# Adding the expert rows into the output in memory by accumulating scatters, with a reordered beginning, in a fused attention and mixture-of-experts kernel

## The reference

```python
x = X                                   # (8, 1024, 128), float32
xn = layernorm(x)
# attention part, per batch and head (16 heads of 64):
q, k, v = xn @ Wq.T, xn @ Wk.T, xn @ Wv.T
q, k = q / max_row_norm(q), k / max_row_norm(k)      # one maximum per batch and head
num = cumsum(v) + q @ cumsum(k outer v);  den = position + q . cumsum(k)
attn = (num / den) @ Wo.T + bo
# expert part: 8 experts, the best 2 for each token
probs = softmax(xn @ router_w);  w1, w2 = top2(probs) / sum(top2(probs))
ffn = sum over the 2 chosen experts e of  w_e * ((silu(xn @ gate_e) * (xn @ up_e)) @ down_e)   # 128 -> 352 -> 128
out = x + attn + ffn
```

## Time and profile before

| | |
|---|---|
| median of 3 runs | 1373.83 us (1367.58 to 1375.96) |
| profiled execution | 1375.33 us, span of its instructions 1373.6 us |
| mean granted TensorE clock | 0.963 of full speed |
| busy share of the span | PE 90%, DVE 68%, ACT 52%, POOL 27% |
| HBM traffic | 28.33 MB read, 24.02 MB written |
| beginning and first group | 0 to 104 us |
| attention | 104 to 1029 us |
| experts | 1029 to 1333 us |
| last stage | 1333 to 1373.6 us |

### The profile page before, as it was taken

How to read it: one execution, slowest core, us unless ns; L and a number is a source line. 1 busy time by engine, 2 the same in 40 slices (tenths; PEclk the granted TensorE clock), 3 DMA queues, 4 the chain that set the end, 5 groups by cost and what they waited for, 6 DMA issues and landing times.

```text
span 1373.6 us, 59302 instructions
## 1 busy us (share of the span) xinstructions
PE 1242.6 (90%) x23920; PEld 1087.7 (79%) x23921; DVE 932.9 (68%) x2662; ACT 708.5 (52%) x1683; POOL 368.6 (27%) x605
## 2 busy tenths in 40 slices
PE   6689999998999999999999999999689999999960
PEld 5468878887887788888788888878579999999960
DVE  6567768776876777787687778667365555555532
ACT  4355656646665654666566466555244444444430
POOL 5300112121111111112111211213523555555546
PEclk9799999999999999999999999999789999999995
DMA  6000000000000000000000000020121222222218
GB/s 212 26 3 6 11 11 17 9 13 13 12 13 10 16 9 13 13 11 13 11 15 10 15 11 11 15 95 18 35 62 52 62 62 61 61 61 62 61 59 348
DMA packets 36324, 55.56 MB, mean 40 GB/s; under 512 B 7600, under 2 KB 26544, under 8 KB 35856
## 3 DMA queue, kind: packets, MB, share of 16 engines
q1 hardware_dynamic: 25744, 29.02, 7.0%
q0 software_dynamic: 9216, 19.17, 4.1%
q10 hardware_dynamic: 1152, 4.19, 0.7%
HBM read 28.33 MB, written 24.02 MB: 38 GB/s over the span
## 4 chain that ended last, share of the span: by engine, by line
PE 70%; DVE 17%; issue 6%; POOL 2%; DMA 2%; ACT 1%; another core or an unknown queue 1%; POOLq 0%; SPq 0%; DVEq 0%; ACTq 0%
PE bank L1142 9%; PE bank L1143 8%; PE bank L1144 8%; PE bank L1312 7%; PE bank L1418 6%; PE bank L1240 6%; PE bank L1292 5%; PE bank L1277 4%; PE bank L1266 3%; PE bank L1179 3%; PE bank L1226 3%; PE bank L1411 3%; PE bank L1302 3%; DVE qs L778 2%; DVE num L849 2%
## 5 line engine op out<-in xcount | busy, mean ns | idle before, releaser
L473 POOL COPY xn<-meta 128x2 f32<-128x2 f32 x128 | 24.9, 195 | 748.6 <-PE bank L1277 747.3
L530 POOL DMA_INDIRECT expert_rows<-yt,wdi x136 | 132.0, 971 | 142.7 <-ACT yt L700 104.3
L575 ACT ACTIVATE kn<-bank 128x512 f32<-128x512 f32 x128 | 69.5, 595 | 192.9 <-PE bank L1226 171.4
L1142 PE MATMUL bank<-xTh,Wh 128*128 128x256 f32 x512 | 154.6, 302 | 2.2 <-DVE xs L772 1.5
L1144 PE MATMUL bank<-xTl,Wh 128*128 128x256 f32 x512 | 147.6, 288 | 5.5 <-issue 5.5
L1143 PE MATMUL bank<-xTh,Wl 128*128 128x256 f32 x512 | 147.4, 288 | 2.1 <-issue 1.8
L593 ACT ACTIVATE qs<-qs,cvec 128x128 f32<-128x128 f32 x480 | 146.1, 395 | 0.7 <-DVE cvec L824 0.2
L1142 PEld LDWEIGHTS bank<-xTh,Wh 128*128 128x128 f32 x512 | 100.4, 196 | 53.0 <-issue 45.6
L1312 PEld LDWEIGHTS bank<-WoT,numT 128*128 128x128 f32 x1024 | 123.1, 193 | 16.1 <-issue 11.7
L477 POOL DMA_INDIRECT sorted_tokens<-xn,slot x128 | 123.4, 964 | 40.5 <-POOL xn L473 29.1
L1312 PE MATMUL bank<-WoT,numT 128*128 128x128 f32 x1024 | 128.8, 279 | 0.8 <-ACT numT L586 0.8
(11 more groups left out here) (214 smaller groups left out, 3024.7 us busy)
## 6 DMA issues: line engine op xcount, KB each, us to landing
xt<-sorted_tokens SPq DMA_DIRECT2D x137, 66.0 KB
er<-expert_rows SPq DMA_DIRECT2D x16, 512.0 KB, 8.3
xa<-in_x SPq DMA_DIRECT2D x8, 512.0 KB, 11.6
out<-ot ACTq DMA_DIRECT2D x8, 512.0 KB, 6.6
gu<-in_gate_up_w SPq DMA_DIRECT2D x1, 2816.0 KB, 11.1
expert_rows<-yt,wdi POOLq DMA_INDIRECT x136
sorted_tokens<-xn,slot POOLq DMA_INDIRECT x128
wraw<-in_wkq SPq DMA_DIRECT2D x2, 512.0 KB, 5.7
```

The lines of the kernel that those rows point to most:

```text
L530: pool.indirect_dma_start(ys_d, bass.IndirectOffsetOnAxis(ap=wdi[:, r:r + 1], axis=0), yt[:, r, :], None).then_inc(f_sc[r], 16)
L1142: pe.matmul(dst, ah, bh, start=start, stop=False)
```

## The change

Four things change, besides the sizes and places of buffers.

1. **Output.** `out` now has the same layout as the expert rows had, and spare rows behind. SP writes the rows of each batch from `xa` to `out` when the batch's attention is complete (`attention_rows`): batches 0 to 5 inside the attention stage, 6 after the expert weights, 7 between the load of tile 0 and the loop that loads the others. The expert loop's scatters then add into these rows (`compute_op=ALU.add`). The barrier and the whole last stage are gone.
2. **Waits of a scatter.** Two experts can add into the same row, and an add reads its row and writes it later. Up to DEEP = 4 scatters of one expert may be in flight; the first scatter of a new expert waits for all before it. Which tiles begin a new expert is only known at run time, so DVE writes a table `tile_w` with the count to wait for, and POOL reads its entry into a register for every tile.
3. **Beginning.** ACT splits the weights in four pieces between its other work. The dummy scatters are 11 of 16 rows in place of 16 of 128. `values_before(0)` moves to j = 1, `sums(0)` and `values_parts(0)` to j = 2. `sums` multiplies by the unsplit `wvraw` once, in every batch, in place of by both parts.
4. **Attention loop.** `choose` is cut in two, at c = 1 and c = 2; `rank_at` is 3 in place of 2 (1 in the last batch, as before). POOL's scatters of sorted rows wait for one group more. At c = 7 DVE copies the four fills ahead of the norm maximum, not behind it.

```diff
+DEEP = 4
-    ys_d = nc.dram_tensor("expert_rows", (K2 * B * N + SPARE * P, D), f32, kind="Internal").ap()
+    spare_d = nc.dram_tensor("spare_rows", (RT * P, D), f32, kind="Internal").ap()
...
+        def landed(r):
+            return 1 if r < RT - DEEP + 1 else 2
...
         def rank_at(b):
-            return 2 if b < B - 1 else 1
+            return 3 if b < B - 1 else 1
...
+            def attention_rows(b):
+                sp.wait_ge(e_y, CB * (b + 1))
+                sp.dma_start(out[b * N:(b + 1) * N, :].rearrange("(p c) d -> p c d", p=P), xa[:, b * CB:(b + 1) * CB, :]).then_inc(o_out, 16)
+            for b in range(B - 2):
+                attention_rows(b)
             sp.wait_ge(a_n, 2 * B * NCP)
             sp.dma_start(gu[:], gate_up_w).then_inc(f_w, 16)
...
+            attention_rows(B - 2)
...
             load_tile(0, 0)
+            attention_rows(B - 1)
             with sp.Fori(0, TILES // RT) as i4:
...
-            for n in range(2):
-                for r in range(RT):
+            for r in range(RT):
+                for n in range(landed(r)):
                     if n > 0:
                         pool.wait_ge(f_sc[r], 16)
-                    pool.indirect_dma_start(ys_d, bass.IndirectOffsetOnAxis(ap=dump[:, r:r + 1], axis=0),
-                                            blank[:, 0, 0:D], None).then_inc(f_sc[r], 16)
+                    pool.indirect_dma_start(spare_d, bass.IndirectOffsetOnAxis(ap=dump[0:16, r:r + 1], axis=0),
+                                            blank[0:16, 0, 0:D], None).then_inc(f_sc[r], 16)
...
+            pool.wait_ge(f_te, 1)
+            pool.wait_ge(o_out, 16 * B)
             with pool.Fori(0, TILES // RT) as i4:
                 for r in range(RT):
                     i = i4 * RT + r
-                    pool.wait_ge(f_sc[r], 16 * (i4 + 2))
+                    pool.wait_ge(f_sc[r], 16 * (i4 + landed(r)))
                     pool.wait_ge(f_wd, ev(1, i))
                     pool.sem_inc(s_pass, 1)
                     pool.tensor_copy(wdi[:, r:r + 1], wd[:, r, 0:1]).then_inc(f_wi, 1)
                     pool.wait_ge(f_wi, ev(1, i))
                     pool.wait_ge(f_yt, ev(1, i))
+                    n4 = (r - DEEP) % RT
+                    pool.wait_ge(f_sc[n4], 16 * (i4 + landed(n4) + (1 if r >= DEEP else 0)))
+                    before_ = pool.value_load(tile_w[0:1, bass.ds(i, 1)], min_val=16, max_val=16 * (TILES // RT + 2))
+                    for n in range(1, DEEP):
+                        more = landed((r - n) % RT) - (1 if r < n else 0) - 1
+                        pool.wait_ge(f_sc[(r - n) % RT], before_ + 16 * more if more else before_)
                     pool.sem_inc(s_pass, 1)
-                    pool.indirect_dma_start(ys_d, bass.IndirectOffsetOnAxis(ap=wdi[:, r:r + 1], axis=0),
-                                            yt[:, r, :], None).then_inc(f_sc[r], 16)
+                    pool.indirect_dma_start(out, bass.IndirectOffsetOnAxis(ap=wdi[:, r:r + 1], axis=0),
+                                            yt[:, r, :], None, compute_op=ALU.add).then_inc(f_sc[r], 16)
...
-                    pool.wait_ge(a_N, 2 * (b * CB + (3 + c if b < B - 1 else 2 + c // 2)) + 1)
+                    pool.wait_ge(a_N, 2 * (b * CB + (4 + c if b < B - 1 else 2 + c // 2)) + 1)
...
             def sums(b):
-                for n, w in enumerate((Wvh, Wvl)):
-                    for par in range(2):
-                        last = pe.matmul(... w[:, 512 * par:512 * par + 512].bitcast(f32), start=(n == 0), stop=(n == 1), ...)
+                for par in range(2):
+                    last = pe.matmul(... wvraw[:, 512 * par:512 * par + 512], start=True, stop=True, ...)
...
                 if c == CB - 1 and more:
-                    norm_max(G, 0)
                     for f in range(4, 8):
                         copy_fill(G, f)
+                    norm_max(G, 0)
                     norm_max(G, 1)
```

More of the change, by code:

```diff
@@ L160, in build @@
         blank2 = place("blank2", [P, E, ROW])
[L162 to L166, removed]
+        assert end_att <= nc.sbuf_usable_end, (end_att, nc.sbuf_usable_end)
         bank = [ctx.enter_context(nc.psum_tensor(f"bank{n}", [P, 512], f32)) for n in range(NB)]
@@ L202, in build @@
             ("xT", "xTh", "xTl", "wd", "wi", "g", "u", "sl", "act", "aT", "aTc", "y", "yt"))
-        o_in, o_out = [sem(f"o_in{n}") for n in range(OB)], [sem(f"o_out{n}") for n in range(OB)]
-        o_a, o_b = sem("o_a"), sem("o_b")
+        o_out = sem("o_out")
         f_ms, f_te = sem("f_ms"), sem("f_te")
@@ L404, in _ @@
                     load_tile(i + 1, (r + 1) % RT)
[L405 to L414, removed]
+            sp.wait_ge(o_out, 16 * B)
         @block.gpsimd
         def _(pool):
-            start_ahead(pool, (o_a, 1), (f_wi, 1))
-            for t in o_out:
-                pool.sem_inc(t, 16)
+            start_ahead(pool, (f_wi, 1))
             pool.memset(ident[:], 0.0).then_inc(s_pool, 1)
@@ L528, in _ @@
                     pool.wait_ge(f_yt, ev(1, i))
+                    n4 = (r - DEEP) % RT
[4 more added lines that the diff above has]
+                        pool.wait_ge(f_sc[(r - n) % RT], before_ + 16 * more if more else before_)
                     pool.sem_inc(s_pass, 1)
-                    pool.indirect_dma_start(ys_d, bass.IndirectOffsetOnAxis(ap=wdi[:, r:r + 1], axis=0),
-                                            yt[:, r, :], None).then_inc(f_sc[r], 16)
+                    pool.indirect_dma_start(out, bass.IndirectOffsetOnAxis(ap=wdi[:, r:r + 1], axis=0),
+                                            yt[:, r, :], None, compute_op=ALU.add).then_inc(f_sc[r], 16)
             for r in range(RT):
[L533 to L539, removed]
+                pool.wait_ge(f_sc[r], 16 * (TILES // RT + landed(r)))
         @block.scalar
@@ L709, in _ @@
                     act.activation(sl[:, s, :], bank[1 + s][:, 0:F], ACT.Silu).then_inc(f_sl, 1)
-                    result(i - 2, (r - 2) % RT, s, i4 + 2 if r >= 2 else i4 + 1)
+                    result(i - 2, (r - 2) % RT, s, i4 + landed((r - 2) % RT) - (1 if r < 2 else 0))
             result(TILES - 2, RT - 2, 0, TILES // RT + 1)
             result(TILES - 1, RT - 1, 1, TILES // RT + 1)
[L713 to L719, removed]
         @block.vector
         def _(dve):
-            start_ahead(dve, (f_xTl, 1), (f_wd, 1), (f_act, 1), (o_b, 1))
+            start_ahead(dve, (f_xTl, 1), (f_wd, 1), (f_act, 1))
             start_ahead(dve, (f_aTc, 1), spare=1)
@@ L862, in state @@
                             dve.wait_ge(z_tail, 16)
-                            for t_ in f_sc:
-                                dve.wait_ge(t_, 32)
+                            for r in range(RT):
+                                dve.wait_ge(f_sc[r], 16 * landed(r))
                             dve.tensor_copy(new, d).then_inc(e_st, 1)
@@ L1055, in _ @@
                 if c == 0 and not more:
-                    choose(b)
+                    choose_first(b)
+                    choose_second()
                 if c == 0:
@@ L1123, in _ @@
             hidden_out(TILES - 1, 1)
-            barrier(dve, 1)
-            with dve.Fori(0, B // OB) as b4:
-                for s in range(OB):
-                    b = b4 * OB + s
-                    dve.wait_ge(o_out[s], 16 * (b4 + 1))
-                    dve.wait_ge(o_a, ev(1, b))
-                    dve.tensor_tensor(ot[:, s], er[:, s, 0], xa[:, bass.ds(b * CB, CB), :], ALU.add).then_inc(o_b, 1)
         @block.tensor
@@ L1323, in _ @@
                     transpose_x(j + 2)
+                if j == 2:
+                    sums(0)
                 if j > 0:
@@ L1328, in _ @@
                 norms(j, 0)
-            sums(0)
             values(0)
@@ L1447, in _ @@
                 down_(n, n % 2, tile_expert(n))
-            barrier(pe, 1)
 def laid_out(inputs):
```

108 lines of the change are left out of this document (61 added, 47 removed).

## The result

The changed kernel takes **1493.23 us** (median of 4 runs, 1491.92 to 1495.64) against 1373.93 us: a ratio of 1.0881, 95% interval 1.0849 to 1.0914. It is 119 us slower; the forecast was 19 us slower, and 1493 lies outside the range of 1345 to 1450 us. The profiled execution took 1491.92 us, its span is 1490.2 us. One execution of a later run, cast_dve_store_act, took 1688 us at a granted clock of 0.65 and is left out of its median.

The account below looks back on a forecast made before the run. PE sets the expert loop's pace at 2.151 us per tile; POOL, with 0.13 us of slack, would become its bound. 1373.8 - 38.4 - 20 + 3 + 64.7 + 9.6 = 1392.7, so 1393 us; range 1345 to 1450.

Parts of the forecast that it names:

- POOL becomes the bound: Expert loop: POOL's period rises from 2.02 to 2.63 us per tile against PE's 2.15, costing 64.7 us.
- The scatter's own duration: Expert loop: an adding scatter takes 0.975 us like a plain one, 0 more, with 0.49 us for the upper end.
- Register load and waits: POOL, ahead of each scatter: address arithmetic, register load, move and four more waits add 0.61 us, all serial (0.31 to 0.93).
- Drains at a change of expert: Expert loop: POOL stands 1.2 us for landings at each of eight changes, 9.6 us in all.
- The end: Behind the last scatter's start: 4.3 us in place of 42.7, a gain of 38.4 us.
- Beginning and attention: Stages ahead of the expert loop: a gain of 12.5 plus 7.5, together 20 us (8 to 28).
- the dummy scatters: Beginning: eleven scatters with an eighth of the rows end PE's late instructions sooner, a gain of 8 us (3 to 11).
- the seven stores: Attention: seven stores of 512 KB beside PE's instruction stream cost about 1 us.
- Start of the expert loop: The load of tile 1, queued on SP behind the last attention rows, comes late: cost 3 us (0 to 5).
- The heavier scatter: Rival, expert loop: 0.49 us more per adding scatter, period 3.12, 1459 us; above 1416 us, with other cases, 0.18.
- the slower register work: Rival, POOL: register load at double SP's duration, 1429 us; above 1416 us, with other cases, 0.18.
- The rival on the other side: POOL between cast and scatter: dispatch runs beside the register load; 1352 or 1318 us; period under 2.39, faster, 0.22.

Follow-up runs that it names:

- cast_dve_store_act: Changed kernel with the cast of the destinations done by DVE and the store of batch 7 issued by ACT; 1318.3 us, ratio 0.961.
- own_rows_add: Changed kernel with adding scatters into a row for each pair of token and expert, without table, register load and drains; 1381.6 us.
- begin_only: Kernel before with the changed beginning and attention loop, old expert loop and last stage; 1348.82 us, ratio 0.9873.

## Why the prediction was wrong, step by step

**POOL becomes the bound: right.** The trace shows each sign that was named: PE idle (30% of the loop, 15 to 20 forecast), ACT and DVE held by POOL, the first scatter at 1019.6 us (1023 forecast). The chain ends in POOL's steps; earlier in the loop the view puts landings (19% of the span) where these steps are, the trap told above. Its slack of 0.13 us per tile was the decisive reading, although the page of the profile gives POOL 27% of the span.

**The scatter's own duration: the step that failed.** The prediction read that the duration is the same for rows of 512 and 528 bytes, concluded that it goes by the number of rows, and took 0 for the add with 0.49 kept for the upper end. It is 0.59 us (1.565 - 0.975), and the prediction's own sign of being wrong, a duration that isn't 0.98 us, came. Both halves were wrong: a scatter of 16 rows still takes 0.85 us, so most of it is fixed, and the add adds mostly to that fixed part. Two scatters with the same number of rows, and 3% apart in bytes, could not tell these apart. 0.59 x 135 = 80 us of the 100 that were missing.

**Register load and waits: mis-sized.** Forecast 0.61 us, measured 0.78 by the run without it and 0.77 in the order of time (1.61 - 0.84). The load itself was well read, 0.30 us against SP's 0.27 and PE's 0.33; the floor of about 600 ns that the Trainium skill gives ("DMA: Bandwidth & Descriptors", section "Latency and other measured facts") does not hold for it on any of the three. What was missing is the range check, 0.17 us with its gaps 0.23, which this form of load brings along. Another (0.78 - 0.61) x 135 = 23 us. Together 103 us, against 100 that the stretch of scatters was longer than forecast (464.4 - 290.5 = 173.9, forecast 74.3).

**Drains at a change of expert:** 1.2 us each were forecast. Ten of the 135 periods are over the median by more than 0.5 us: nine of 4.00 to 4.21 us and one of 5.46, together 8.5 us over it (9.6 forecast). Two of the ten are not due to drains: own_rows_add, which has none, is late at the same two tiles (3.26 and 4.61 us against its 2.59). The other eight come to 5.7 us, 0.7 each: POOL reached its waits later than forecast, and so less of the landing was left to wait for.

**The end:** 6.2 us behind the last scatter's start (4.3 forecast). The add lands after 3.3 us (3.0 forecast).

**Beginning and attention:** PE's first transposition of the expert loop moved from 1029.0 to 1005.7 us, 23 us (20 forecast); by medians these parts gave 18.5 us in begin_only, and 22 and 25 in the two variants with 11 scatters of 128 rows and 16 of 16. In the sum the dummy scatters stood with 8 us and measured 12 to 15; all the other terms stood with 12 and measured 10 (1371.8 - 1361.6), not told apart. No run shows the 1 us that was put for the seven stores. **Start of the expert loop:** 13.9 us from there to the first scatter in place of 11.5 (2.4 more, forecast 3). Tile 1 is one part of it: its transposition starts 4.0 us behind the first one in place of 2.7, 1.35 us later. PE in order of time, of the kernel after, then of the kernel before:

```profile
1005.72 0.33 PE L1394 MATMUL bank<-ident,xt 128*128 128x128 f32 x1 [0.39 <-DVE xa L864]
...
1009.74 0.33 PE L1394 MATMUL bank<-ident,xt 128*128 128x128 f32 x1 [0.69 <-DMA xt<-sorted_tokens]
```

```profile
1031.67 0.27 PE L1399 MATMUL bank<-ident,xt 128*128 128x128 f32 x1
```

**The rivals.** The heavier scatter was one of them, with 0.49 us more and 1459 us; it came with nearly that size, and together with the slower register work, where the prediction had counted only one of the two at a time. Both unknown costs stood on the same serial chain, so their upper ends had to be added for the range: 3.12 + 0.32 = 3.44 us gives 1502 us. A range up to there would have held the result. The rival on the other side was also real as a mechanism: the dispatch can run beside other work, but not while a cast of its own engine stands between. In the run with the cast on DVE it does, and the time is 1319 us, the 1318 named for that case.

## What to carry to other kernels

Before giving an engine one more instruction per turn, write down its shortest turn, from a place where it was catching up, and what in it waits for its own results. A busy share misleads here: POOL at 54% of the stage had 6% of slack. And when several unknown prices fall on one serial chain, add their upper ends, or better, take out the link that makes the chain serial: that was worth 174 us, without making any of the steps that stayed shorter.

## What the runs showed of the hardware that was not expected

An adding scatter costs 0.48 us more than an overwriting one at 16 rows and 0.60 at 128, and lands 3.3 us after its start in place of 2.2. POOL's dispatch of a scatter, 0.75 us from the last semaphore instruction to the scatter's start in the changed kernel's loop, disappears beside a running scatter (0.30 us from one to the next). And PE's instructions come to a near standstill for 14 us while POOL issues 16 scatters of 128 rows at 0.30 us from each other (28 instructions from 38 to 54 us); with 11 of them and three pauses for landings, or 16 of 16 rows and eight pauses, PE executes 73 and 76 there, and the kernel is 12 to 15 us faster.
